# Second layer of a two-layer kernel rewritten in steps of one sequence: scores once, exponentials per head, row sums on VectorE, probabilities transposed on TensorE

## What is computed

```python
def _L1_cond_ref(x, emb, src_mask, ...):          # H = 16 heads of 32, T = 128, D = 512
    xn = layer_norm(x, norm_w, norm_b)
    q = (xn @ q_w + q_b).reshape(Bx, Tx, H, -1)
    k = (xn @ k_w + k_b).reshape(Bx, Tx, H, -1)
    att = jnp.einsum('bnhl,bmhl->bnmh', q, k)
    att = att + (1.0 - mask) * -1000000.0
    att = jax.nn.softmax(att, axis=2)
    v = ((xn @ v_w + v_b) * src_mask[:, :, None]).reshape(Bx, Tx, H, -1)
    y = jnp.einsum('bnmh,bmhl->bnhl', att, v).reshape(Bx, Tx, Dx)
    e = jax.nn.silu(emb) @ emb_w + emb_b
    scale, shift = jnp.split(e[:, None, :], 2, axis=2)
    h = layer_norm(y, sb_norm_w, sb_norm_b) * (1.0 + scale) + shift
    return x + jax.nn.silu(h) @ out_w + out_b
```

## Time and profile before

| | before |
|---|---|
| median of 3 runs | 2157.12 us (2156.51 to 2157.31) |
| the profiled execution's own time | 2159.14 us |
| its span | 2157.0 us |
| mean granted clock of TensorE | 0.997 |
| PE busy | 2122.9 us (98%) |
| PE weight loads | 1861.9 us (86%) |
| DVE busy | 1399.9 us (65%) |
| ACT busy | 909.0 us (42%) |
| POOL busy | 572.4 us (27%) |
| DMA | 86.47 MB, 40 GB/s on average |

### The profile page before, as it was taken

One profiled execution on the slowest core, in us unless ns is written; L12 is line 12 of the kernel. 1 busy time (PEld: TensorE's weight loads), 2 busy tenths in 40 slices (PEclk: granted clock), 3 DMA queues, 4 the chain that ended last, 5 costly groups with the idle time before them and its releaser, 6 DMA issues.

```text
span 2157.0 us, 53563 instructions
## 1 busy us (share of the span) xinstructions
PE 2122.9 (98%) x20955; PEld 1861.9 (86%) x20955; DVE 1399.9 (65%) x2986; ACT 909.0 (42%) x2088; POOL 572.4 (27%) x899
## 2 busy tenths in 40 slices
PE   7999999999999999999999999999999999999997
PEld 4888888888888888887989898989898888888886
DVE  6777777777777777766665656565555555555554
ACT  3323333333333333343444444444544444445444
POOL 4233332233332333333222222221212121212120
PEclk9999999999999999999999999999999999999999
DMA  6211010111001110013000000000101010101000
GB/s 209 108 39 39 28 36 34 39 39 39 25 34 39 39 39 30 33 35 118 21 24 34 29 30 29 29 31 28 38 21 39 20 39 20 39 20 39 20 31 21
DMA packets 52165, 86.47 MB, mean 40 GB/s; under 512 B 5667, under 2 KB 14565, under 8 KB 52134
## 3 DMA queue, kind: packets, MB, share of 16 engines
q1 hardware_dynamic: 52118, 86.03, 11.3%
q10 hardware_dynamic: 16, 0.00, 0.0%
HBM read 52.32 MB, written 33.69 MB: 40 GB/s over the span
## 4 chain that ended last, share of the span: by engine, by line
PE 96%; DVE 2%; ACT 1%; DMA 0%; issue 0%; SPq 0%; POOL 0%; DVEq 0%; ACTq 0%
PE bank L541 14%; PE bank L542 14%; PE bank L543 13%; PE bank L550 9%; PE bank L551 8%; PE bank L552 8%; PE bank L1675 5%; PE bank L1701 3%; PE bank L1128 3%; PE bank L1707 3%; PE bank L1718 2%; PE bank L1116 2%; PE bank L1014 1%; PE bank L1641 1%; PE bank L1038 1%; PE bank L1042 1%
## 5 line engine op out<-in xcount | busy, mean ns | idle before, releaser
L550 PE MATMUL bank<-xT_hi,w_hi 128*128 128x256 f32 x1536 | 452.2, 294 | 1.1 <-DVE top L1347 1.1
L551 PE MATMUL bank<-xT_lo,w_hi 128*128 128x256 f32 x1536 | 446.1, 290 | 0.0
L552 PE MATMUL bank<-xT_hi,w_lo 128*128 128x256 f32 x1536 | 442.9, 288 | 0.0
L541 PE MATMUL bank<-w_hi,xT_hi 128*128 128x512 f32 x768 | 306.9, 400 | 4.4 <-DVE bias_all L402 4.4
L550 PEld LDWEIGHTS bank<-xT_hi,w_hi 128*128 128x128 f32 x1536 | 291.1, 190 | 18.8 <-issue 7.7
L543 PE MATMUL bank<-w_lo,xT_hi 128*128 128x512 f32 x768 | 301.3, 392 | 0.0
L542 PE MATMUL bank<-w_hi,xT_lo 128*128 128x512 f32 x768 | 300.9, 392 | 0.0
L551 PEld LDWEIGHTS bank<-xT_lo,w_hi 128*128 128x128 f32 x1536 | 291.6, 190 | 2.0 <-issue 0.8
L552 PEld LDWEIGHTS bank<-xT_hi,w_lo 128*128 128x128 f32 x1536 | 292.0, 190 | 0.0
L541 PE MATMUL bank<-w_hi,h_hi 128*128 128x512 f32 x512 | 216.8, 423 | 5.8 <-DVE h_lo L1389 3.7
L934 ACT ACTIVATE heads<-bank,k_neg 128x128 f32<-128x128 f32 x256 | 70.0, 370 | 355.5 <-DVE k_neg L799 355.5
(11 more groups left out here) (210 smaller groups left out, 4051.3 us busy)
## 6 DMA issues: line engine op xcount, KB each, us to landing
xr<-in_x SPq DMA_DIRECT2D x32, 512.0 KB, 3.4
x_between_layers<-ends SPq DMA_DIRECT2D x64, 256.0 KB, 2.0
xr<-x_between_layers SPq DMA_DIRECT2D x32, 512.0 KB, 3.6
out<-ends SPq DMA_DIRECT2D x64, 256.0 KB, 2.0
store<-in_L_cond_W_emb SPq DMA_DIRECT2D x4, 1024.0 KB, 11.7
mask_rows<-mask_parts SPq DMA_DIRECT2D x128, 2.0 KB
heads<-in_L_cond_emb_w SPq DMA_DIRECT2D x2, 1024.0 KB, 8.0
store<-in_L_cond_emb_w SPq DMA_DIRECT2D x2, 1024.0 KB, 12.1
```

The source lines that it names most:

```text
L541: yield nc.tensor.matmul(bank[:, :], a_hi[:, c, b, :], w_hi[:, m, c, :], start=(c == 0), stop=False)
L550: yield nc.tensor.matmul(dst, w_hi[:, m, c, fs], a_hi[:, c], start=(first and c == 0), stop=False)
L551: yield nc.tensor.matmul(dst, w_hi[:, m, c, fs], a_lo[:, c], start=False, stop=False)
L552: yield nc.tensor.matmul(dst, w_lo[:, m, c, fs], a_hi[:, c], start=False, stop=(last and c == C - 1))
```

## The change

The second layer is rewritten. Pairs are still loaded and projected two sequences at a time, but from the scores on everything goes in steps of one sequence (`step0` and `step1` of a pair), on each engine.

- The scores are made once. `exps` now reads them from the same banks with the queries on the partitions, takes each head by itself (128x128, 16 instructions a sequence), and its bias is the head's negative maximum. `shift_row`, `shift_out`, `weight_scores`, `mask_column` and the ones column are gone.
- `totals` (new, DVE) sums the probabilities over the keys, four heads an instruction, out of SBUF; `end_outputs` takes its reciprocal from there.
- `prob_turned` (new, PE) transposes the probabilities of each head into the score banks (16 transposes a sequence), and `prob_out` (new, ACT) copies them to SBUF, four heads an instruction. `mixed` multiplies them with v; the sums' product is gone.
- `turned` has four transposes for a sequence instead of five. All engines' orders are new; step1 of pair i holds the query and key projections of pair i+1.
- SP issues the load of pair i+2 ahead of the second store of pair i-1. The embedding's weights go to other buffers, with other waits.

The core of the diff:

```diff
-        emb[1].room([m.heads[:, 0:C * D], m.heads[:, C * D:2 * C * D], m.store[0][:], m.store[1][:]], m.store[2][:])
+        emb[1].room([m.store[0][:], m.store[1][:], m.store[2][:], m.gates[:]], m.store[0][:])
...
-    QK_BANKS = ((0, 1), (2, 3))
-    W_BANKS = (4, 5, 6, 7)
-    Y_BANKS = ((4, 5), (6, 7))
-    V_BANKS = (4, 6)
-    S_BANKS = (0, 1, 2, 3)
-    S_ORDER = ((0, 1, 2, 3), (2, 3, 0, 1))
-    Z_BANKS = (5, 4)
-    O_BANKS = (5, 4)
-    X_BANKS = (7, 6)
-    T_BANKS = (7, 0)
+    Y_BANK, Z_BANK, O_BANK = 4, 7, 6
+    QK_BANKS, V_BANKS, X_BANKS = (5, 6), (5, 6), (5, 7)
+    FIRST_QK_BANKS, FIRST_V_BANKS = ((0, 1), (2, 3)), (4, 6)
+    LAST_Z_BANK, LAST_O_BANK = 5, 0
...
         def body(i, first, more, last):
             if not first:
                 store(i - 1, 0)
-                store(i - 1, 1)
-                sp.wait_ge(s["stored"], seq(16 * PAIR, i - 1, 16 * PAIR))
+                sp.wait_ge(s["out"], seq(PAIR, i - 1, PAIR))
             if more:
                 sp.wait_ge(x_in, seq(16, i, 32))
                 load_rows(sp, x1_d, xr, i + 2, slot_of(i + 2), x_in)
+            if not first:
+                sp.dma_start(out[(i - 1) * PAIR + 1], y_out[:, 1]).then_inc(s["stored1"], 16)
...
-        sp.wait_ge(s0["y_ps"], PAIR * NP)
+        sp.wait_ge(s["lo_qk"], 2)
         emb.load(sp, (0, 1))
-        sp.wait_ge(s["lo_qk"], 2)
-        emb.load(sp, (2, 3))
+        sp.wait_ge(s0["silu"], PAIR * NP)
+        emb.load(sp, (3,))
+        sp.wait_ge(s["lo_vo"], 1)
...
         def body(i, first, more, last):
             if not first:
-                biases(i, slot_of(i), False)
-            if not last and not first:
-                norm(i + 1)
-            if not first:
-                end_rstd(i - 1, 0)
-                end_gains(i - 1)
                 end_rstd(i - 1, 1)
-            mask_column(i, first)
+                gains_of(i, False)
+            if not last:
+                if not first:
+                    pool.wait_ge(s["h_lo"], seq(PAIR, i - 1, PAIR))
+                value_bias(i + 1, False)
+            end_rstd(i, 0)
+            if first:
+                gains_of(0, True)
+            if more:
+                norm(i + 2)
+                pool.wait_ge(s["h_lo"], seq(PAIR, i, 1))
+                residual(i + 2, slot_of(i + 2))
...
+        def totals(i, b, some):
+            for a in some:
+                dve.wait_ge(s["prob"], seq(PAIR * C, i, b * C + a + 1))
+                nc.vector.reduce_sum(total[:, b, C * a:C * a + C], prob[:, a], AX_X).then_inc(s["total"], 1)
...
+        def step0(i, last):
+            maxima(i, 0, (0, 1, 2))
+            end_outputs(i - 1, 1)
+            maxima(i, 0, (3,))
+            end_add(i - 1, slot_of(i - 1), 0)
+            totals(i, 0, (0,))
+            end_norm(i - 1, 1)
+            totals(i, 0, (1,))
+            values(i, 0)
+            totals(i, 0, (2, 3))
+            end_silu(i - 1, 1)
+            values(i, 1)
+            low_part(i - 1, 1)
             if not last:
                 x_low(i + 1, 0)
                 x_low(i + 1, 1)
...
+            end_add(i - 1, slot_of(i - 1), 1)
...
+        def step1(i, first, more, last):
+            maxima(i, 1, (0, 1, 2))
+            end_outputs(i, 0)
+            maxima(i, 1, (3,))
+            if first:
+                emb.leave_bank(dve, ps[Z_BANK])
+            if not last:
+                keys_out(i + 1, (0, 1))
+            totals(i, 1, (0,))
+            end_norm(i, 0)
+            totals(i, 1, (1,))
+            if first:
+                emb.gains(dve)
+            if not last:
+                keys_out(i + 1, (2, 3))
+            if more:
+                row_stats(i + 2, slot_of(i + 2))
+            totals(i, 1, (2, 3))
+            end_silu(i, 0)
+            if more:
+                norm(i + 2, slot_of(i + 2))
+            low_part(i, 0)
+            if first:
+                low(O)
...
-        def exps(prev, b, banks):
...
+        def exps(i, b, first):
             for a in range(HC):
+                act.wait_ge(s["top"], seq(PAIR * C, i, b * C + a + 1))
+                if a == 0 and not (first and b == 0):
+                    act.wait_ge(s["total"], seq(PAIR * C, i, b * C))
+                for c in range(C):
+                    last = nc.scalar.activation(prob[:, a, c, :], ps[a][:, c * P:(c + 1) * P], ACT.Exp,
+                                                bias=top[:, b, C * a + c:C * a + c + 1])
+                last.then_inc(s["prob"], 1)
+
+        def prob_out(i, b, some):
+            for a in some:
+                act.wait_ge(s["pT_ps"], seq(PAIR * C, i, b * C + a + 1))
+                nc.scalar.activation(prob_T[:, a], ps[a][:, :].rearrange("p (c t) -> p c t", c=C),
+                                     ACT.Copy).then_inc(s["pT"], 1)
...
+        def step0(i, first, last):
+            if not first:
+                copy_yT(i - 1, 1)
+            exps(i, 0, first)
+            if not first:
+                gate(i - 1, 1)
+                tanh(i - 1, 1)
+            prob_out(i, 0, (0,))
+            if not first:
+                h_high(i - 1, 1)
+            prob_out(i, 0, (1, 2, 3))
+            if not last:
+                x_high(i + 1, 0)
+                x_high(i + 1, 1)
+
+        def step1(i, first, last):
+            copy_yT(i, 0)
+            exps(i, 1, first)
+            gate(i, 0)
+            tanh(i, 0)
+            if not last:
+                queries_out(i + 1, (0, 1))
+            prob_out(i, 1, (0,))
+            h_high(i, 0)
+            prob_out(i, 1, (1, 2, 3))
+            if not last:
+                queries_out(i + 1, (2, 3))
...
-        def weight_scores(prev, b, banks):
...
-            for a in range(HC):
-                rows = slice(DH * a, DH * a + C)
-                nc.tensor.matmul(ps[banks[a]][:, :], one_rows[rows, :],
-                                 top_T[rows, b].rearrange("p c t -> p (c t)"), start=True, stop=False,
-                                 tile_position=(DH * a, 0))
-            heads(banks, K, Q, b, range(HC), s["w_ps"])
...
-        def mixed(prev, b, exps_done):
...
-            for c in range(C):
-                for a in range(HC):
-                    last = nc.tensor.matmul(ps[Y_BANKS[b][1]][DH * a:DH * a + DH, 0:P], one_col[:, c, :],
-                                            prob[:, b, HC * c + a, :], start=(c == 0), stop=(c == C - 1),
-                                            tile_position=(0, DH * a))
-            last.then_inc(s["yT_ps"], 1)
...
-        def shift_row(i, b):

-            pe.wait_ge(s["top"], seq(PAIR * C, i, C * (b + 1)))
-            nc.tensor.transpose(ps[T_BANKS[b]][:, 0:P], top[:, b, :], ident[:]).then_inc(s["top_ps"], 1)
...
+        def prob_turned(i, b, some):
+
+            for a in some:
+                pe.wait_ge(s["prob"], seq(PAIR * C, i, b * C + a + 1))
+                for c in range(C):
+                    last = nc.tensor.transpose(ps[a][:, c * P:(c + 1) * P], prob[:, a, c, :], ident[:])
+                last.then_inc(s["pT_ps"], 1)
+
+        def mixed(i, b, first):
+
+            pe.wait_ge(s["v"], seq(PAIR, i, b + 1))
+            if b == 1:
+                pe.wait_ge(s["y"], seq(PAIR, i, 1))
+            elif not first:
+                pe.wait_ge(s["y"], seq(PAIR, i - 1, PAIR))
+            pe.wait_ge(s["pT"], seq(PAIR * C, i, C * (b + 1)))
+            for c in range(C):
+                for a in range(HC):
+                    last = nc.tensor.matmul(ps[Y_BANK][DH * a:DH * a + DH, c * P:(c + 1) * P],
+                                            v[:, b, HC * c + a, :], prob_T[:, a, c, :], start=True, stop=True,
+                                            tile_position=(0, DH * a))
+            last.then_inc(s["yT_ps"], 1)
...
+        def turned(prev, b):
+
+            pe.wait_ge(s["yT"], seq(PAIR, prev, b + 1))
+            for c in range(C):
+                last = nc.tensor.transpose(ps[Y_BANK][:, c * P:(c + 1) * P], yT[:, c, :], ident[:])
+                if c == C - 1:
+                    last.then_inc(s["y_ps"], 1)
+                yield
...
+        def step0(i, last):
+            scores(i, 0)
+            woven(out_rows(i - 1, 0), turned(i - 1, 1))
+            run(value_rows(i, 0))
+            z_transposed(i - 1, 1)
+            prob_turned(i, 0, (0, 1))
+            pe.wait_ge(s["out"], seq(PAIR, i - 1, 1))
+            run(value_rows(i, 1))
+            prob_turned(i, 0, (2, 3))
+            if not last:
+                pe.wait_ge(s["v"], seq(PAIR, i, 1))
+                x_transposed(i + 1, 0)
+                pe.wait_ge(s["g"], seq(PAIR, i - 1, PAIR))
+                x_transposed(i + 1, 1)
+            pe.wait_ge(s["v"], seq(PAIR, i, PAIR))
+            run(out_rows(i - 1, 1))
+            mixed(i, 0, False)
+
+        def first_step0():
+            scores(0, 0)
+            pe.wait_ge(s0["x1"], PAIR * NP)
+            x_transposed(1, 0)
+            x_transposed(1, 1)
+            pe.wait_ge(s["v"], PAIR)
```

(83 more changed lines are left out.)

395 lines of the change are left out of this document (126 added, 269 removed).

## The result

The changed kernel takes 2119.19 us (median, 2118.06 to 2120.77) against 2156.92 us for the kernel before on the same chip: a ratio of 0.9822, 95% interval 0.981 to 0.9834. The forecast was 2130 with a range of 2112 to 2160, and its rival A, in which PE never waits, was 2118. So the direction and the mechanism held, and the gain, 37.7 us, is 11 us more than forecast. The profiled execution took 2118.06 with a span of 2116.2.

A forecast was written before the change was run, and what follows sets the result against it. PE (TensorE), busy for all of the loop's pass, was taken as the bound. Pass 1 at 1044.2, 30 passes of 34.45 us, 16.3 and 35.9 gave a span of 2129.9, so 2130 (range 2112 to 2160).

The forecast's parts named there:

- rival A: In the loop, PE never waits: 0 us of waits a pass, 2118 us; chance 0.14 with a little beyond.
- PE bounds, the others have room: Second layer's loop: PE busy for all of a 35.55 us pass; DVE and ACT rise to 25 of 34.
- Work removed: PE per pass: weight scores 3.04 us, row sums by matmuls 1.53, four transposes 0.44.
- Work added: PE per pass: 32 transposes of 128x128 probabilities at 0.11 us each, 3.52; net of removed work -1.49.
- Waits: PE inside a pass: 0.1 to 0.2 us for z in each step, queries' copy 0.1 late; 0.4 a pass.
- The walk: Both steps timed from the first score matmul: z at 7.6 and 7.8 us, PE there at 7.5 and 7.65.
- ScalarE: ACT in the loop: exponentials 8.3 us, eight copies 8 x 0.6, at most 25 of 34; not the bound.
- The ends: Outside the 30 passes: pass 1 begins at 1044.2 us (+/-4); pass 31's first step 16.3, then 35.9.
- slack of only 0.3 at h_lo: First step of a pass: h_lo ready at 12.9 to 13.3 us, wanted by PE at 13.5.
- B: In both steps, late z holds PE: even at 1.3 us of waits a pass, 2163 at 1.5; chance 0.10.
- C: In the loop, transposes cost 0.13 to 0.14 us: +0.9 a pass, 2157; chance 0.15 shared with waits 0.9 to 1.3.
- D: Clock falls once a pass around the run of 16 transposes: 3 us a pass, 2220 us; chance 0.03.

The follow-up runs named there:

- run 1: Changed kernel with each of the 32 transposes of probabilities of a pass made twice: 2225.31 us, pass 37.50.
- run 5: Kernel before, with the 16 products of query and key left out of the weight scores: 2104.28 us, pass 33.77.
- run 6: Kernel before, with the row-sum matmuls cut to a quarter (one chunk of four): 2117.36 us, pass 34.24.
- run 10: Changed kernel with the first sequence's mixed products moved between its eighth and ninth output products, away from the scores: 2125.6 us, pass 34.23.
- run 3: Changed kernel with z's normalization moved ahead of the first sum of probabilities in both steps: 2112.52 us, pass 33.83.
- run 2: Changed kernel with one extra DVE addition of 128x512 ahead of z's normalization in both steps: 2158.51 us, pass 35.25.
- run 4: Changed kernel with one extra ACT copy of 128x512 behind the exponentials of each step: 2119.54 us, pass 34.03.

## Why the prediction was right, and where it was off

- **PE bounds, the others have room.** Right. Runs 1, 5 and 6 change PE's work by +3.47, -1.78 and -1.31 a pass and move the spans by 31 times as much (run 6 2116.0 against 2157.0: 41).
- **Work removed.** Forecast 3.04 + 1.53 + 0.44. Of the weight scores the products are 1.78 (run 5); the four-row matmuls were not run alone. The sums are 1.75 (run 6) where I credited 1.53, because I charged the mixed blocks that stay with 0.23 of entering and leaving each. Side by side with the scores they cost 1.01 and not 1.11, 0.20 a pass, which fits what run 10 shows of a change saved. This is the term of the sum that was mis-sized; the order of the new program, which was in the diff, could have told it: each mixed block stands directly ahead of scores.
- **Work added.** 0.11 a transpose forecast, 0.1085 measured (run 1): 0.05 a pass. Both together, 0.25, are about the 0.23 by which PE's own work (33.83) is below 34.06. What was put for the four-row matmuls and the four transposes that went holds by this remainder only.
- **Waits.** Forecast 0.4: z 0.3 and the queries 0.1. Measured 0.20 for z (run 3). For the queries there is none to be seen: from mixed to scores are 1.01 us ahead of the step that needs their copy (1519.03 to 1520.04) and 1.01 ahead of the one that doesn't (1502.30 to 1503.31). 0.2 a pass less.
- The sum: 0.20 + 0.05 + 0.2 = 0.45 against the 0.42 between 34.45 and 34.03, times 30.
- **The walk** put z at 7.6 and PE at 7.5 in the first step. The trace has z written 7.43 behind the scores' start (1520.04), and PE ready for it at 7.44, where it starts in kernel 3. In the second step they are 7.61 for 7.8 and 7.62 for 7.65. So each figure was up to 0.2 high. PE waits for z all the same, since 0.05 lies between the writing and the start and the block behind such a start takes 0.06 more. A walk of some fifteen durations can't place two arrivals nearer than that, and run 2 shows what hangs on it: up to the whole gain.
- **ScalarE** at nothing: right, with room for at least one more copy a step (run 4).
- **The ends.** The start was right within 0.7 us. In the last pass's first step I took the missing transposes of xn off as 0.87 and forgot what they cover: PE then waits 0.7 for h_lo, which is written 0.14 us ahead of need in the other passes. That row was part of my own walk ("slack of only 0.3 at h_lo"). The tail (34.3 for 35.9) is right by two errors that partly cancel: the last products start 25.5 behind the last scores, not 28, and from them to the end are 8.7 us, not 7.8.
- **Rivals.** A came nearest in time, but by luck: waits exist (0.20 a pass), and PE's own work is smaller by about as much. B is real, with its threshold near where it was put, and the changed kernel stays clear of it because the addition, sum and copies ahead of z end just when PE arrives. C falls by the 1.75 us for sixteen transposes and by run 1, D by run 1.

## What to carry to other kernels

Where one engine is busy for all of a loop, price an edit by the distances between starts around the same kind of block, and count for every small block what it stands beside: moving it can be worth as much as a shorter instruction. Then walk the order of the other engines up to each thing the busy engine waits for; work that is free by an engine's sum is free only behind the last such point, and the cheapest improvement is to put what the bound engine needs ahead of what nobody waits for yet. In a tail the same holds for the order of waits on one queue: an operation that waits for late work must not stand ahead of the chain that ends last.

## What the hardware showed that I had not expected

A wait of 0.1 us ahead of a matmul block has no row among PE's waits. It was seen as 0.66 in the place of 0.60 for four transposes and as 0.04 in the distance ahead of them, and proven only by taking it away (run 3).

The embedding's small DVE operations (`emb.gains`) take longer beside work of GpSimd. In the kernel before, some of them ran beside GpSimd's additions of 128x512; in the changed kernel GpSimd does nothing then. Timeline of DVE and POOL in the kernel before, and of DVE in the changed one:

```profile
1026.15 2.56 POOL L1260 TENSOR_TENSOR xr<-xr,bias_all 128x512 f32 x2 [22.84 <-DVE top L1347]
...
1026.16 1.35 DVE L529 TENSOR_SCALAR half_gain<-store,vec 128x64 f32<-128x64 f32 x1
1027.44 1.36 DVE L531 SCALAR_TENSOR_TENSOR store<-store,vec 128x64 f32<-128x64 f32 x1
1028.72 0.24 DVE L529 TENSOR_SCALAR half_gain<-store,vec 128x64 f32<-128x64 f32 x1
...
1029.08 1.06 DVE L529 TENSOR_SCALAR half_gain<-store,vec 128x64 f32<-128x64 f32 x1
```

```profile
1033.56 0.24 DVE L522 TENSOR_SCALAR half_gain<-store,vec 128x64 f32<-128x64 f32 x1
1033.73 0.27 DVE L524 SCALAR_TENSOR_TENSOR store<-store,vec 128x64 f32<-128x64 f32 x1
```

The same operation takes 0.24 us alone and 1.35 beside one of GpSimd's. Four instructions are that long, and each ends 0.05 to 0.08 us behind the GpSimd addition that it runs beside, as if it had waited for the whole of it. The eight from 1025.81 to 1031.22 took 5.4 us in the kernel before and 1.5 in the changed one. It isn't so for every pair: in the loop of the changed kernel x's low part, which reads a PSUM bank and SBUF, runs beside GpSimd's additions in every pass and keeps its 0.69 us:

```profile
1533.71 2.04 POOL L1263 TENSOR_TENSOR v_bias<-bias_all,mask_now 128x512 f32<-128x512 f32 x2
...
1533.88 1.29 DVE L1324 TENSOR_TENSOR xT_lo<-bank,xT_hi 128x512 fp32r<-128x512 f32 x2 [0.69 <-ACT xT_hi L1507]
```

That the small operations and GpSimd's share a way to SBUF would fit, but no run here takes GpSimd's additions away or moves them. It happens once and not in the loop.
